# Seeding the mask tile just ahead of the next exponential instead of just behind the last one

## What is computed

```
xn  = layernorm(x)
out = x + encoder(xn) + experts(xn)

encoder: 4 layers of
    h = h + mha(layernorm(h))        # 16 heads of 8, causal mask and ALiBi bias
    h = h + W2 gelu(W1 layernorm(h)) # hidden size 512
  then a last layernorm
experts: one layer of attention, 8 heads of 16, no mask, with
  projections that use fewer features for later tokens
```

## The kernel before

| place in the slot | ScalarE's steps |
|---|---|
| start | E(0,0), E(0,1), then `at+` (L769: `attnt`, waits for the transposes of `at`), E(0,2) |
| group 1 | E(1,0), `xt+` (L747: `xnt` from the first norm), E(1,1), E(1,2), `qk+` (L754: two halves of `y`) |
| group 2 | E(2,0), E(2,1), E(2,2) |
| group 3 | E(3,0), `xt2+` (L774: `xnt` from the second norm), E(3,1), E(3,2), `f1+` (L781: four Gelu's, between two table loads) |

## Time and profile before

### The profile page before, as it was taken

The page is one execution under the profiler, slowest core; times in us unless marked ns, Lnnn a source line. Parts: engine busy times, 40 slices in busy tenths (PEclk is TensorE's granted clock), DMA queues, the critical chain, the costliest instruction groups (busy, mean ns, idle before and its releaser), DMA issues. The chain is left out here.

```text
span 1736.1 us, 40658 instructions
## 1 busy us (share of the span) xinstructions
PE 1505.9 (87%) x12256; PEld 1117.8 (64%) x12256; DVE 1127.6 (65%) x3106; ACT 1218.8 (70%) x2165; POOL 517.9 (30%) x907
## 2 busy tenths in 40 slices
PE   0777777489999989999999899999998999999995
PEld 0444554267777767777777677777776777677763
DVE  6567775356667656666666566666666667767762
ACT  3233333167888878888888788888887888878874
POOL 5222221112232222222333232322222234444433
PEclk9999999689999999999999999999999999999998
DMA  4333332222222222222222223222222222222220
GB/s 115 98 92 109 95 105 62 73 82 76 81 75 73 73 79 73 90 73 73 73 80 82 63 77 91 80 76 76 76 83 67 77 89 85 73 81 79 83 59 10
DMA packets 109892, 137.21 MB, mean 79 GB/s; under 512 B 14272, under 2 KB 95808, under 8 KB 109824
## 3 DMA queue, kind: packets, MB, share of 16 engines
q1 hardware_dynamic: 102176, 115.81, 23.5%
q0 software_dynamic: 7680, 20.98, 3.4%
HBM read 70.54 MB, written 65.01 MB: 78 GB/s over the span
## 5 line engine op out<-in xcount | busy, mean ns | idle before, releaser
L761 ACT ACTIVATE probs<-exp_ps 128x512 f32<-128x512 f32 x896 | 523.8, 590 | 388.9 <-PE exp_ps L876 388.1
L628 DVE TENSOR_REDUCE negm<-mxp 128x2 f32<-128x512 f32 (+1 forms) x1152 | 610.3, 568 | 186.0 <-PE mxp L855 151.2
L849 PE MATMUL mxp<-kst_l,qbd_l 127*128 127x256 f32 x2048 | 405.5, 309 | 45.8 <-DMA qbd_l<-split_L 40.7
L849 PEld LDWEIGHTS mxp<-kst_l,qbd_l 127*128 127x128 f32 x2048 | 355.4, 197 | 90.5 <-DMA qbd_l<-split_L 61.7
L876 PE MATMUL exp_ps<-qbd_l,kst_l 128*128 128x512 f32 x768 | 364.9, 489 | 33.2 <-ACT exp_ps L785 28.7
L785 ACT ACTIVATE exp_ps<-masktf 128x512 f32<-128x512 f32 x513 | 308.8, 602 | 22.7 <-DVE rest L696 6.5
L454 POOL TENSOR_SCALAR veps<-mv 128x2 f32<-128x2 f32 x144 | 31.8, 221 | 909.3 <-DVE mv L586 906.1
L855 PE MATMUL mxp<-maskb,identb 128*128 128x256 bf16 x1024 | 294.3, 287 | 0.0
L899 PE MATMUL pvp<-probs,vst_l 128*32 128x256 f32 (+1 forms) x4096 | 219.5, 332 | 0.1
L876 PEld LDWEIGHTS exp_ps<-qbd_l,kst_l 128*128 128x128 f32 x768 | 143.5, 193 | 88.3 <-ACT exp_ps L785 39.6
L674 DVE COPY ost<-pvp 128x512 f32<-128x512 f32 x80 | 55.3, 691 | 207.6 <-PE pvp L899 207.6
(11 more groups left out here) (91 smaller groups left out, 1855.0 us busy)
## 6 DMA issues: line engine op xcount, KB each, us to landing
split_L<-hi SPq DMA_DIRECT2D x256, 128.0 KB, 2.1
kst_l<-split_L SPq DMA_DIRECT2D x64, 384.0 KB
qbd_l<-split_L SPq DMA_DIRECT2D x256, 96.0 KB
split_L<-lo POOLq DMA_DIRECT2D x128, 128.0 KB, 2.1
split_F<-hi SPq DMA_DIRECT2D x64, 128.0 KB, 2.1
kst_f<-split_F SPq DMA_DIRECT2D x16, 384.0 KB, 3.8
qbd_f<-split_F SPq DMA_DIRECT2D x32, 192.0 KB, 4.4
split_F<-lo POOLq DMA_DIRECT2D x32, 128.0 KB, 2.4
```

The lines of the kernel that those rows point to most:

```text
L628: dve.tensor_reduce(negm[:, s, qt, h0:h0 + 2], mxp[:, (plan.max_chunks * g + ch) % 3, :].rearrange("p (h t) -> p h t", h=2)[:, :, 0:keys], ...
L761: act.activation(probs[:, g[0], ch, :], exp_ps[:, (plan.exp_chunks * g[0] + ch) % 2, :], ACT.Exp, scale=plan.scale).then_inc(q.b_exp, 1)
L849: last = pe.matmul(mxp[:, bank, k * T:(k + 1) * T], qbd[plan.name][0:MAX_ROW, s, h, qt * P:(qt + 1) * P], kst[plan.name][0:MAX_ROW, s, g[0 ...
```

## The change

The seed is taken from behind the exponential that frees its bank, and put ahead of the next exponential of the unit. The wait for `b_exp` is on the same value, and the number of seeds is the same.

```diff
@@ -757,12 +757,12 @@
                         G, ch = GROUPS * u + g[0], g[1]
                         if ch == 0:
                             wait_past(act, q.b_pv, G - GROUPS + 1)
+                        if plan.causal and ch > 0:
+                            act.wait_ge(q.b_exp, plan.exp_chunks * G + ch)
+                            seed((plan.exp_chunks * g[0] + ch - 1) % 2)
                         act.wait_ge(q.b_s, plan.exp_chunks * G + ch + 1)
                         act.activation(probs[:, g[0], ch, :], exp_ps[:, (plan.exp_chunks * g[0] + ch) % 2, :], ACT.Exp,
                                        scale=plan.scale).then_inc(q.b_exp, 1)
-                        if plan.causal and ch < 2:
-                            act.wait_ge(q.b_exp, plan.exp_chunks * G + ch + 1)
-                            seed((plan.exp_chunks * g[0] + ch) % 2)
                     elif step == "at+" and plan.causal:
                         act.wait_ge(q.c_at, u + 1)
                         wait_past(act, q.c_op, u - 1)
```

## The result

The changed kernel takes 1760.78 us (median of 4 runs, 1759.01 to 1768.15), the kernel before 1737.04 us (median of 4). The ratio is 1.0137 with a 95% interval of 1.0108 to 1.0167, so between 19 and 29 us slower. The prediction said 1755 us and 1.1%, with a range of 1747 to 1764 us. Over more runs, 55 of the kernel before that stand beside the experiments (two at a far lower clock, of 1933 and 2124 us, left out) and 21 of the changed one, the medians are 1736.2 and 1760.2 us, 24.0 apart.

The account below looks back on a forecast made before the run. TensorE, busy 87% of the span, was the engine to look at. 63 slots x 0.31 us = 19.5, less 1, gave +18.5 on 1736.2: 1755 us, 1.1% slower, range 1747 to 1764 us.

Parts of the forecast that it names:

- The seed that is waited for is S(3,0), and it alone matters: Of three moved seeds, TensorE already waits for that of group 3, chunk 0; moving the other two costs nothing.
- over a microsecond to spare: Seed of group 0, chunk 1, moved behind `attnt`: ends about 922.7, its score matmul starts at 923.97.
- The seed starts 0.95 us behind E(3,0), 0.31 to 0.32 late: On ScalarE, exponential to `xnt` 0.50 us plus `xnt` to seed 0.45, where exponential to seed was 0.63.
- The bound without overlap (0.55): Upper bound on the group 3 seed's delay if ScalarE's instructions don't overlap: 0.55 us; as the dearer move +35 us, chance 0.08.
- M(0,2) moves from S(0,0) to TensorE's own order: Next slot's score matmul of group 0, chunk 2 starts 0.13 us behind `at`, no longer 0.05 behind its seed.
- The transfer isn't a cushion: `negt` and queries' stack transfers hang on group 3's delayed score matmul, so the stack lands the same 0.31 us late.
- 18 slots give back some 1 us in all: Where the stack's transfer may not come last, up to 0.11 us each returns; counted as 18 x 0.05 us.
- this sign: In TensorE's wait list, the waits for the stacked queries should stay near 21 us.
- The sum: Over the encoder's slots: 63 x 0.31 = 19.5 us, less some 1 us given back, so +18.5 us.
- Faster, because ScalarE paces the slot: Rival: ScalarE's chain sets the slot's length, 0.13 us less in each of 63 slots, -8 us, 1728 us; chance 0.06.
- the 0.11 of slack: TensorE is held some 0.11 us for a seed at the next slot's score matmul of group 0, chunk 2.

Follow-up runs that it names:

- the dose: Kernel before, with the seed of group 3, chunk 0 put behind `xnt` and also behind the group's next exponential: 1788.16 us, ratio 1.0298.
- S(3,0) alone: Kernel before, with only the seed of group 3, chunk 0 moved behind `xnt` of the second norm: 1761.08 us against 1736.67, ratio 1.0126.
- `pv` first: Kernel before, seeds unmoved, with TensorE doing `pv` of group 2 ahead of the score matmul of group 3, chunk 2: 1755.64 us, ratio 1.0074.
- the keys first: Changed kernel, with SyncE issuing the stacked keys and their waits ahead of the `negt` transfer: 1727.55 us, ratio 0.9934 to the kernel before.

## Why the prediction held, point by point

- **The seed that is waited for is S(3,0), and it alone matters.** Right, and shown: alone it brings a ratio of 1.0126, the other two leave the wait as it was. Their room was smaller than "over a microsecond to spare": the moved S(0,1) ends 1.10 us ahead of M(1,0) in the median slot and 0.61 in the tightest of 60, the moved S(1,0) 1.01 us or more ahead of M(1,2).
- **The seed starts 0.95 us behind E(3,0), 0.31 to 0.32 late.** Measured 0.94, so 0.31. The bound without overlap (0.55) didn't occur.
- **M(0,2) moves from S(0,0) to TensorE's own order.** Right: 0.14 behind `at`, 0.42 behind the seed's end.
- **The transfer isn't a cushion.** Right, and shown by the dose: 0.82 us late cost 52 us. The mean from M(3,2) to the first maximum matmul of the next slot, over 60 slots of the timelines, is 8.43 us before and 8.42 after, and both transfers are issued as far behind M(3,2) as before.
- **18 slots give back some 1 us in all.** Too small to be seen: 8.42 says nothing came back, the 8.38 of S(3,0) alone says up to 3 us. (The stretch of the wait list holds 61 slots and not 62, so it would be 17.) The stack's waits didn't stay near 21 us but rose to 27, so this sign failed. From M(3,2) to M(0,2) the mean fell from 7.57 to 7.48 us, and from M(0,2) to the first maximum matmul it rose from 0.86 to 0.94: TensorE, no longer held at M(0,2), waits that much longer for the stack. The hidden wait turned into a visible one.
- **Size.** The sum was +18.5; the 59 slots show 20.4, the stretch ahead of them 4 less. The measured medians differ by 23.7, whose interval of 19 to 29 us reaches nearly down to the sum. In the profiles 7 us of the difference lie in the expert branch, where the prediction had nothing, and go with the granted clock. Expert units of 16.7 us or more (from the second to the fifteenth), at a mean granted clock of 0.90 (one at 0.83), number six in the changed kernel, five in S(3,0) alone and in the larger dose, three in `pv` first, and two or fewer in all other profiles; the first seed comes at 312 to 314 us in the first three, at 308 in the fourth, at 302 to 307 in the others. The late S(3,0) by itself doesn't bring that: with the keys first it is as late, TensorE's order is unchanged, and the first seed comes at 305 us. Whether some of the 24 us in the medians comes this way stays open: one profile of each kernel can't say it, and over all runs the mean granted clock is 0.970 before and 0.969 after. So the mechanism was right and the size in the slots is the forecast one; that the total stayed within the range although some 5 us of it have no place in the sum is the range's doing.
- **Faster, because ScalarE paces the slot**, the rival of the other sign: wrong for this kernel, since M(3,2) was 0.31 late, more than the 0.11 of slack. With M(3,2) covered, its first half came true (M(0,2) held by S(0,0)) and its gain still didn't reach the end, for the stack's wait took it.

## What to carry to other kernels

Before an instruction is moved in an engine's queue, look for who waits for it: of three seeds that went behind another instruction, two had about a microsecond of cover left and cost nothing that could be seen, and one was already waited for and passed its 0.31 us on in each slot. A wait ahead of the instruction that releases the next slot's transfer had no cushion here, although TensorE waited for that transfer: both are the same chain. And a wait that is removed is a gain only if nothing else then leaves later: the same 0.36 us of seed wait cost 13 us when its cover was put ahead of `negt`, and gained 17 us when M(3,0) was moved forward instead.

## What the runs showed of the hardware

- A seed that has to wait for the end of the exponential ahead started 0.02 to 0.04 us behind that end; `y` or `xnt`, which don't depend on it, started 0.10 to 0.11 us ahead of it (0.60 long, 0.49 to 0.50 to the next start). The seed copy, from SBUF to PSUM, let the next one in only 0.06 to 0.09 us ahead of its end (0.60 long, 0.51 to 0.54 to the next start). A table load behind an exponential started at its end (0.59 to 0.60 to the next start).
- M(3,2) started 0.05 us behind the end of the seed that released it in the median slot, before and after, and 0.15 at most.
- The transfer of 16 KB (the row of maxima) landed 2.2 us after its issue (median) when nothing had been issued in its queue for some 3 us or more, and 3.2 us after when 384 KB were issued 0.7 us ahead of it in the same queue.
- Taking the waits from ahead of the keys' transfer shortened the queue's idle time from 0.42 to 0.06 us (mean) but lengthened the transfer's own issue from 0.33 to 0.57 us.
- With the same 79 matmuls, an expert unit took 15.4 us at a granted clock of 1.00 (2.4 GHz) and 17.0 us at a mean of 0.90, so partly at the lower level (1.2 GHz).
